# The projections and the scan of a two-layer kernel as one program without a barrier between them

## The chip, the cores and the metric

One Trainium2 chip; the kernel runs on 1 core of it. The metric is the time of one execution on the device in microseconds (us), lower is better. "Engines" are TensorE (PE, its weight loads PEld), VectorE (DVE), ScalarE (ACT), GpSimd (POOL) and SyncE (SP, which here only issues transfers).

## What is computed

Two layers, each a selective state-space mixer (Mamba) and a mixture of experts, both added to the rows `x` (4 x 512 rows of 512). Both mixers read the same context (4 x 512 x 256), so their projections can all be made at the start. For one mixer and batch:

```
x    = in_proj_w @ context                       # 512 channels x 512 positions
u    = silu(conv4(x) + conv_b)                   # 4 taps along the positions
dt, Bm, Cm = split(x_proj_w @ u)                 # 16 + 16 + 16 rows
delta = softplus(dt_proj_w @ dt + dt_proj_b);  A = -exp(A_log)
state = state * exp(delta * A) + (delta * u) * Bm   # 16 states a channel, along the positions
y    = (sum over the states of state * Cm + D * u) * silu(z)
```

z comes from the layer norm of `x`, whose mean and variance are read at the start too. After the first mixer come routing, experts and the second layer.

## The kernel before

`stage_proj` makes the projections: 8 rounds `n` (`ORDER`: layer 1's four batches, then layer 0's), each of 4 channel tiles `j`. For a tile PE multiplies (L267) into banks 0 to 3, ACT copies it with padding (`COPY`, L313) and makes the first tap (L316), DVE the three other taps (L351), ACT the tanh (L305), DVE `u` (L344), and PE adds its share of `x_proj` into `XD` (bank 4, L277). PE runs the products of round n+1 between those of round n. When a round is whole, ACT copies `XD` to `xds` (L301) during the next round, and SP writes its rows to `bc_d`. Behind the last round DVE negates `An` (L361) and makes the layer-norm statistics of the 16 row tiles (`dve_stats`, L633 to L638); POOL makes the reciprocal roots of them (`pool_rstd`, L642 to L649). Then all engines meet: `clear_semaphores` frees the semaphores, with a barrier.

`scan_stage` does 32 groups `g` (mixer, batch, channel tile) of 16 states `i`. For each state ACT makes `dA` (L525), POOL `dBu` (L560), DVE the scan (L607) and then the product with C of the state before (L591), PE sums with an identity matrix (L471) into `YS` (bank 4). POOL and ACT may run a few states ahead of the scan (POOL has two `dBu` buffers). A group's softplus is made during the group before: `dt_proj` on PE (L459), seven activations on ACT (`prep`, steps 0 to 2, L504 to L515) with a table load for `Ln`, `pool_poly` (L536), `dve_pick` (L575), `pool_delta` (L540), `pool_du` (L546). Group 0's has no group before it and stands alone at the start of the stage. SP loads B and C of a batch in four chunks each (L417, L418) out of `bc_d` into `big`, where the context lay. All orders are written out by hand, one program an engine; nothing is reordered. `side` (the class `Beside`) adds the layer-0 experts' work to the scan's steps.

Of the kernel before, what the change touches and what calls it, by code (L numbers as in the profile page):

```python
# [25 lines left out]
ALU = mybir.AluOpType  # L26
ACT = mybir.ActivationFunctionType
# [75 lines left out]
def program(nc, x, ctxT, mix, moe0, moe1, out):  # L103
    ctx = ExitStack()
    with ctx:
# [101 lines left out]
        def stage_proj():  # L207
# [6 lines left out]
            x1_out, bc_out, chain, expa, pad0 = sem("p_x1_out"), sem("p_bc_out"), sem("p_chain"), sem("p_exp_a"), sem("p_pad0")  # L214
            stat_done, mean_done, rstd_done = sem("p_stat"), sem("p_mean"), sem("p_rstd")
            tap_done = sem("p_first_tap_done")
            XP, XD = bank[0:4], bank[4]
            with nc.Block() as block:
                @block.sync
                def _(sp):  # L220
                    def in_proj(k):
                        sp.dma_start(winT[k], mix[k]["in_proj"].rearrange("(c p) e -> p c e", p=P)).then_inc(win_in[k], 16)

                    def ctx(b):
                        sp.dma_start(cx[:, b, :, :], ctxT[b].rearrange("(c p) l -> p c l", p=P)).then_inc(ctx_in[b], 16)

                    def conv(k):
                        sp.dma_start(cw[k][:, :, :], mix[k]["conv_w"].rearrange("(j p) w -> p j w", p=P)).then_inc(par_in[k], 16)
                        sp.dma_start(cbias[k][:, :], mix[k]["conv_b"]).then_inc(par_in[k], 16)
                        sp.dma_start(xprT[k], mix[k]["x_proj"].rearrange("(j p) r -> p j r", p=P)).then_inc(par_in[k], 16)  # L230

                    in_proj(1)
                    ctx(0)
                    conv(1)
                    conv(0)
                    for b in range(1, B):
                        ctx(b)
                    in_proj(0)
                    for k in (0, 1):
                        sp.dma_start(An[k][:, :, :], mix[k]["A_log"].rearrange("(j p) n -> p j n", p=P)).then_inc(late_in[k], 16)  # L240
                        for t_sb, t_d in ((dtb, "dt_b"), (dsk, "D")):
                            sp.dma_start(t_sb[k][:, :], mix[k][t_d]).then_inc(late_in[k], 16)
                    sp.wait_ge(pad0, 4)
                    sp.dma_start(dtwT[0:NR, :], mix[0]["dt_proj"]).then_inc(late_in[0], 16)
                    sp.dma_start(X[:, :, :], x.rearrange("(t p) d -> p t d", p=P)).then_inc(x_in, 16)
                    for n, (k, b) in enumerate(ORDER):
                        if k == 1:
                            sp.wait_ge(u_done, (n + 1) * NJ)
                            sp.dma_start(u1_d[b], Y[:, b * NJ:(b + 1) * NJ, :]).then_inc(u_out[b], 16)
                        sp.wait_ge(xds_done, n + 1)  # L250
                        sp.dma_start(bc_d[b + k * B], xds[NR:NR + 2 * NS, b, :]).then_inc((bc_out, x1_out)[k], 16)
                        if k == 1:
                            sp.dma_start(dt1_d[b], xds[0:NR, b, :]).then_inc(x1_out, 16)
                    sp.wait_ge(bc_out, 16 * B)
                    sp.wait_ge(late_in[0], 64)

                @block.tensor
                def _(pe):
                    def in_proj(n, j):
                        k, b = ORDER[n]  # L260
                        if j == 0 and b == 0:
                            pe.wait_ge(win_in[k], 16)
                        if j == 0 and k == 1:
                            pe.wait_ge(ctx_in[b], 16)
                        at_least(pe, xpad_done, n * NJ + j - 3 if n else 0)
                        for c in range(DC):
                            last = nc.tensor.matmul(XP[j][:, :], winT[k][:, c, j * P:(j + 1) * P], cx[:, b, c, :],  # L267
                                                    start=c == 0, stop=c == DC - 1)
                        last.then_inc(xp_done, 1)

                    def x_proj(n, j):
                        k, b = ORDER[n]
                        if j == 0:
                            at_least(pe, xds_done, n)
                            pe.wait_ge(par_in[k], 48)
                        pe.wait_ge(u_done, n * NJ + j + 1)
                        nc.tensor.matmul(XD[0:48, :], xprT[k][:, j, :], Y[:, b * NJ + j, :], start=j == 0,  # L277
                                         stop=j == NJ - 1).then_inc(xd_done, 1)

                    for j in range(NJ):  # L280
                        in_proj(0, j)
                    for n in range(2 * B):
                        for j in range(NJ):
                            if n < 2 * B - 1:
                                in_proj(n + 1, j)
                            x_proj(n, j)

                @block.gpsimd
                def _(pool):
                    nc.gpsimd.memset(dtwT[:, :], 0.0).then_inc(pad0, 1)  # L290
                    nc.gpsimd.memset(xds[:, :, :], 0.0).then_inc(pad0, 1)
                    pool_rstd(pool, mean_done, rstd_done)

                @block.scalar
                def _(act):
                    def copy_xd(n):
                        k, b = ORDER[n]
                        act.wait_ge(xd_done, (n + 1) * NJ)
                        if n == B:
                            act.wait_ge(x1_out, 32 * B)  # L300
                        nc.scalar.copy(xds[0:48, b, :], XD[0:48, :]).then_inc(xds_done, 1)  # L301

                    def tanh(n, j):
                        act.wait_ge(conv_done, n * NJ + j + 1)
                        nc.scalar.activation(cth[j % 2], cv[j % 2], ACT.Tanh).then_inc(th_done, 1)  # L305

                    act.wait_ge(pad0, 4)
                    act.wait_ge(chain, 4)
                    for n, (k, b) in enumerate(ORDER):
                        for j in range(NJ):  # L310
                            act.wait_ge(xp_done, n * NJ + j + 1)
                            at_least(act, conv_done, n * NJ + j - 1)
                            nc.scalar.copy(xpad[j % 2][:, 3:3 + L], XP[j][:, :]).then_inc(xpad_done, 1)  # L313
                            act.wait_ge(xpad_done, n * NJ + j + 1)
                            at_least(act, u_done, n * NJ + j - 1)
                            nc.scalar.activation(cv[j % 2], xpad[j % 2][:, 0:L], ACT.Identity, bias=cbias[k][:, j:j + 1],  # L316
                                                 scale=cw[k][:, j, 0:1]).then_inc(tap_done, 1)
                            if j:
                                tanh(n, j - 1)
                            if j == 1 and n:  # L320
                                copy_xd(n - 1)
                        tanh(n, NJ - 1)
                        if n == B:
                            for i in range(2):
                                act.wait_ge(late_in[i], (64, 48)[i])
                                nc.scalar.activation(An[i][:, :, :], An[i][:, :, :], ACT.Exp).then_inc(expa, 1)
                    copy_xd(2 * B - 1)

                @block.vector
                def _(dve):  # L330
                    for i in range(2):
                        nc.vector.memset(xpad[i][:, 0:3], 0.0).then_inc(pad0, 1)
                    link = Chain(dve, chain)
                    for k in (1, 0):
                        dve.wait_ge(par_in[k], 48)
                        link(nc.vector.tensor_scalar_mul(cw[k][:, :, :], cw[k][:, :, :], 0.5))
                        link(nc.vector.tensor_scalar_mul(cbias[k][:, :], cbias[k][:, :], 0.5))

                    def u_of(n, j):
                        k, b = ORDER[n]  # L340
                        dve.wait_ge(th_done, n * NJ + j + 1)
                        if k == 0 and j == 0:
                            dve.wait_ge(u_out[b], 16)
                        nc.vector.scalar_tensor_tensor(Y[:, b * NJ + j, :], cth[j % 2], 1.0, cv[j % 2],  # L344
                                                       ALU.add, ALU.mult).then_inc(u_done, 1)
# [1372 lines left out]
```

## Time and profile before

| | before |
|---|---|
| median of 3 runs | 2302.93 us (2299.14 to 2305.75) |
| profiled execution | 2298.09 us, span 2296.4 us |
| PE / DVE / ACT / POOL busy | 1920.6 / 1415.4 / 846.8 / 984.7 us |
| the projections | span's start to 118.5 us |
| statistics, barrier, group 0's softplus | 118.5 to 150.8 us |
| scan | 150.8 us to about 1400 us, experts beside its second half |

The profile is one execution; its spans count from its first instruction. In each 1/40 of the span, DVE is at 0.6 to 0.9 busy or more through the projections and the scan, PE at 0.9 or more in the last third.

### The profile page before, as it was taken

Reading aid. Unit: us, or ns where it says so; the run is one execution under the profiler, and the core shown is the slowest. Engines: PE = TensorE matmul, PEld = TensorE weight load, DVE = VectorE, ACT = ScalarE, POOL = GpSimd, SP = SyncE. Lnnn points to the kernel's source line nnn. Section 1 sums busy time; section 2 is a strip of 40 time slices with the busy share of each in tenths; the row PEclk is TensorE's granted clock in tenths of the full one; section 3 lists DMA queues with packets and bytes.
Section 4 is the critical chain, followed back from the end, with each engine's and each line's share of the span. In section 5 each row is a group of like instructions: output and inputs, shape, how many; then the busy total and the mean of one; then the engine's idle time right before and its main releaser. Section 6 shows DMA issues by size and latency. Waiting matters only on the chain. (4 is left out here: it accounts for less than half of the span.)

```text
span 2296.4 us, 18644 instructions
## 1 busy us (share of the span) xinstructions
PE 1920.6 (84%) x5075; PEld 877.6 (38%) x5075; DVE 1415.4 (62%) x1958; ACT 846.8 (37%) x1372; POOL 984.7 (43%) x873
## 2 busy tenths in 40 slices
PE   8836678789788795489999984999999999999980
PEld 2201133234233341134444433454455555555540
DVE  6869998899898889697888884654111111111114
ACT  5645554545454543655555541110111111111110
POOL 0047866676666665886877762212300000000005
PEclk9958899999899997599999996999999999999995
DMA  5069500302203003568678645113645554455457
GB/s 192 25 233 212 185 13 10 147 14 77 116 13 125 36 10 159 174 210 343 231 253 341 215 166 211 55 38 98 217 157 172 185 176 155 172 184 179 156 194 224
DMA packets 102256, 348.57 MB, mean 152 GB/s; under 512 B 15184, under 2 KB 16208, under 8 KB 84112
## 3 DMA queue, kind: packets, MB, share of 16 engines
q1 hardware_dynamic: 94480, 322.27, 40.9%
q0 software_dynamic: 7680, 25.17, 3.3%
q8 instruction: 41, 0.67, 0.1%
q14 instruction: 55, 0.45, 0.1%
HBM read 284.88 MB, written 62.52 MB: 151 GB/s over the span
## 5 line engine op out<-in xcount | busy, mean ns | idle before, releaser
L560 POOL TENSOR_TENSOR work<-work,big 128x512 f32<-128x512 f32 x512 | 658.1, 1291 | 231.6 <-DVE bank L607 229.9
L471 PE MATMUL bank<-work,ident 128*128 128x512 f32 x928 | 528.5, 683 | 213.2 <-DVE work L591 162.6
L607 DVE TENSOR_TENSOR_SCAN bank<-bank,work 128x512 f32<-128x512 f32 x512 | 625.4, 1221 | 102.3 <-ACT bank L525 54.5
L525 ACT ACTIVATE bank<-work,An 128x512 f32<-128x512 f32 x512 | 346.3, 690 | 305.3 <-DVE work L591 302.3
L471 PEld LDWEIGHTS bank<-work,ident 128*128 128x128 f32 x928 | 173.3, 209 | 512.6 <-DVE work L591 335.1
L591 DVE TENSOR_TENSOR work<-bank,big 128x512 f32<-128x512 f32 x512 | 344.7, 673 | 9.5 <-PE bank L471 9.3
L1636 POOL DMA_INDIRECT W<-ys_d,slot x32 | 32.1, 1002 | 624.7 <-PEq L1623 615.3
L1593 PE MATMUL bank<-Y,big 128*128 128x512 f32 x528 | 258.7, 594 | 0.0
L1183 DVE SCALAR_TENSOR_TENSOR work<-work,bank 128x352 f32<-128x352 f32 (+1 forms) x62 | 35.9, 579 | 300.0 <-ACT work L1173 299.9
L959 PE MATMUL bank<-W,work 128*128 128x512 f32 x384 | 190.8, 600 | 0.0
L1161 ACT COPY work<-bank 128x512 f32<-128x512 f32 x62 | 36.3, 586 | 379.7 <-PE bank L1146 379.7
L1607 PE MATMUL bank<-big,W 128*128 128x512 f32 x352 | 168.3, 592 | 0.0
L1593 PEld LDWEIGHTS bank<-Y,big 128*128 128x128 f32 x528 | 98.6, 191 | 82.7 <-issue 57.5
L1146 PE MATMUL bank<-work 128*128 128x512 f32 (+1 forms) x234 | 114.4, 601 | 4.5 <-DMA work<-down_last 4.5
L1188 DVE SCALAR_TENSOR_TENSOR work<-work,bank 128x352 f32<-128x352 f32 (+1 forms) x62 | 36.0, 580 | 123.3 <-PE bank L1135 123.2
L1135 PE MATMUL bank<-work 128*128 128x352 f32 x312 | 110.7, 460 | 1.5 <-DMA work<-up 1.5
L1544 ACT ACTIVATE work<-bank 128x512 f32<-128x512 f32 x44 | 26.3, 597 | 221.9 <-PE bank L1593 221.9
L1125 PE MATMUL bank<-work 128*128 128x352 f32 x312 | 106.0, 464 | 2.3 <-DMA work<-gate 2.3
L959 PEld LDWEIGHTS bank<-W,work 128*128 128x128 f32 x384 | 72.8, 194 | 84.5 <-issue 84.5
L1498 DVE SCALAR_TENSOR_TENSOR W<-work,bank 128x512 f32<-128x512 f32 x44 | 30.2, 686 | 94.9 <-PE bank L1593 94.7
L1135 PE MATMUL bank<-W,work 128*128 128x512 f32 x184 | 88.2, 618 | 0.5 <-DMA W<-up 0.5
L1607 PEld LDWEIGHTS bank<-big,W 128*128 128x128 f32 x352 | 65.2, 190 | 58.7 <-issue 46.0
(245 smaller groups left out, 2284.5 us busy)
## 6 DMA issues: line engine op xcount, KB each, us to landing
big<-bc_d SPq DMA_DIRECT2D x64, 1024.0 KB, 6.7
work<-gate SPq DMA_DIRECT2D x39, 704.0 KB, 4.1
work<-up SPq DMA_DIRECT2D x39, 704.0 KB, 4.1
W<-gate SPq DMA_DIRECT2D x23, 1024.0 KB, 4.8
W<-up SPq DMA_DIRECT2D x23, 1024.0 KB, 5.4
W<-down SPq DMA_DIRECT2D x23, 1024.0 KB, 5.4
work<-down SPq DMA_DIRECT2D x39, 512.0 KB, 3.7
work<-xs_d SPq DMA_DIRECT2D x62, 256.0 KB, 4.3
```

The lines of the kernel that those rows point to most:

```text
L471: nc.tensor.matmul(YS[:, :], ident[:, :], hC[ring(g * NS + u[0])], start=v == 0, stop=v == len(units[g]) - 1).then_inc(sum_done, 1)
L525: nc.scalar.activation(H[i % 4][:, :], delta[g % 2], ACT.Exp, scale=An[vb // B][:, g % NJ, i:i + 1]).then_inc(dA_done, 1)
L560: nc.gpsimd.tensor_tensor(dBu[i % 2], du[g % 2], Bb[:, i, :], ALU.mult).then_inc(dBu_done, 1)
L591: nc.vector.tensor_tensor(hC[ring(s)], H[i % 4][:, :], Cb[:, i, :], ALU.mult).then_inc(hC_done, 1)
L607: nc.vector.tensor_tensor_scan(H[i % 4][:, :], H[i % 4][:, :], dBu[i % 2], 0.0, ALU.mult, ALU.add).then_inc(scan_done, 1)
L959: ins = nc.tensor.matmul(dst[:, :], at[:, c * P:(c + 1) * P], w[:, c, :], start=c == 0, stop=c == DK - 1)
L1125: ins = nc.tensor.matmul(self.G[:, 0:self.F], self.xT[q][:, c * P:(c + 1) * P], self.wg[:, c, :], start=c == 0, stop=c == DK - 1)
L1135: ins = nc.tensor.matmul(self.U[:, 0:self.F], self.xT[q][:, c * P:(c + 1) * P], self.wu[:, c, :], start=c == 0, stop=c == DK - 1)
L1146: ins = nc.tensor.matmul(self.TB[:, :], self.hT[0:fn, c * P:(c + 1) * P], self.wd[0:fn, c, :], start=c == 0, stop=c == len(self.chunks) - 1)
L1161: nc.scalar.copy(self.yo, self.TB[:, :]).then_inc(S["yo_done"], 1)
L1593: ins = nc.tensor.matmul(dst[:, :], sgu[:, c, u // DK * FS + f * P:u // DK * FS + (f + 1) * P], xTb[b][:, c, :], start=c == 0, stop=c == D ...
L1607: ins = nc.tensor.matmul(down_bank(b, r)[:, :], hT[c][:, r * P:(r + 1) * P], sdw[:, c, :], start=c == 0, stop=c == NF - 1)
```

## The change

The projections are no block of their own any more. `projections()` returns one function for each engine, and the scan's program of that engine calls it first; the block's end, the clearing of semaphores and the barrier go. `XD` moves from bank 4 to bank 5, so that `YS` is free. What orders the two parts now are waits on semaphores of the projections (`free`).

- Group 0's softplus stands inside the projections: `dt_proj(0)` and the three `prep` steps behind round 5 (`mid` on PE and ACT), `pool_poly(0)`, `pool_delta(0)` and `pool_du(0)` right behind POOL's two memsets, `dve_pick(0)` behind round 6.
- The layer-norm statistics stay on DVE between the projections and the scan; `rstds` goes on POOL behind the fourth `dBu` of group 0.
- SP issues the first B and C chunks behind its last `bc_d` write, once every `in_proj` product has read the context; each later batch's chunks wait for that batch's `bc_d` row.

```diff
-            XP, XD = bank[0:4], bank[4]
-            with nc.Block() as block:
+            XP, XD = bank[0:4], bank[5]
...
             def tensor(pe, mid):
                 for n in range(2 * B):
                     for j in range(NJ):
                         if n < 2 * B - 1:
                             in_proj(n + 1, j)
                         x_proj(n, j)
+                    if n == B + 1:
+                        mid(pe)
...
             def gpsimd(pool):
                 nc.gpsimd.memset(xds[:, :, :], 0.0).then_inc(pad0, 1)
-                    pool_rstd(pool, mean_done, rstd_done)
...
             def scalar(act, mid):
                     tanh(n, NJ - 1)
+                    if n == B + 1:
+                        mid(act)
...
             def vector(dve, mid):
                     u_of(n, NJ - 1)
+                    if n == B + 2:
+                        mid(dve)
...
+            def free(eng, name):
+                if name == "sp big":
+                    eng.wait_ge(xp_done, 2 * B * NJ)
+                if name == "sp W":
+                    eng.wait_ge(xd_done, 2 * B * NJ)
+                    eng.wait_ge(u_done, 2 * B * NJ)
...
+                if name == "pe":
+                    eng.wait_ge(xds_done, B + 1)
+                    eng.wait_ge(late_in[0], 64)
+                if name == "act":
+                    eng.wait_ge(chain, 4 + 2 * B * NJ * (NTAP - 2) + 2)
+                if name == "act gates":
+                    eng.wait_ge(rstd_done, 5)
...
             def loads(sp):
+                proj_sp(sp)
+                free(sp, "sp big")
+                sp.wait_ge(bc_out[0], 16)
                 for c in range(4):
                     chunk(0, c)
+                free(sp, "sp W")
                 side.before("sp", sp)
...
             def tensor(pe):
-                dt_proj(0)
+                def first_step(pe):
+                    free(pe, "pe")
+                    dt_proj(0)
+
+                proj_pe(pe, first_step)
...
             def scalar(act):
-                for step in range(3):
-                    prep(0, step)
+                def first_step(act):
+                    for step in range(3):
+                        prep(0, step)
+
+                proj_act(act, first_step)
+                free(act, "act")
...
             def gpsimd(pool):
+                proj_pool(pool)
                 pool_poly(pool, 0)
                 pool_delta(pool, 0)
                 pool_du(pool, 0)
...
                     nc.gpsimd.tensor_tensor(dBu[i % 2], du[g % 2], Bb[:, i, :], ALU.mult).then_inc(dBu_done, 1)
+                    if g == 0 and i == 3:
+                        rstds(pool)
...
             def vector(dve):
-                dve.wait_ge(poly_done, 1)
-                dve_pick(0)
+                def first_step(dve):
+                    dve.wait_ge(poly_done, 1)
+                    dve_pick(0)
+
+                proj_dve(dve, first_step)
+                stats(dve)
...
         stage_setup()
-        stage_proj()
-        clear_semaphores()
         scan_stage(Beside(moe0))
```

ACT where round 5 ends and round 6 begins, in the program before (bank0 and bank1 hold the products of round 6's first tiles, `W` the padded tiles, taps and tanh):

```order
L305 ACTIVATE W<-W 128x512 [waits p_conv_done] x2
L313 COPY W<-bank0 128x512 [waits p_conv_done,p_xp_done]
L316 ACTIVATE W<-W,cbias0,cw0 128x512 [waits p_u_done,p_xpad_done]
L313 COPY W<-bank1 128x512 [waits p_conv_done,p_xp_done]
L316 ACTIVATE W<-W,cbias0,cw0 128x512 [waits p_u_done,p_xpad_done]
L305 ACTIVATE W<-W 128x512 [waits p_conv_done]
```

The same place in the changed program, whose line numbers are 4 lower here (`s_dt_done` is signalled by `dt_proj`, `s_dt_read` by the second activation):

```order
L301 ACTIVATE W<-W 128x512 [waits p_conv_done] x2
L541 ACTIVATE work<-bank4,dtb0 128x512 [waits s_dt_done]
L542 ACTIVATE work<-bank4,dtb0 128x512
L545 ACTIVATE work<-work 128x512 [waits s_dt_read]
L548 ACT_TABLE_LOAD
L548 ACTIVATE work<-work 128x512 [waits s_exp_done]
L549 ACTIVATE work<-work,pbias 128x512
L550 ACTIVATE work<-work,pbias 128x512
L552 ACTIVATE work<-work,pbias 128x512 [waits s_square_done]
L309 COPY W<-bank0 128x512 [waits p_conv_done,p_xp_done]
L312 ACTIVATE W<-W,cbias0,cw0 128x512 [waits p_u_done,p_xpad_done]
```

Seven activations and a table load now stand between the last tanh of round 5 and the first copy of round 6; a second table load follows ahead of round 6's first tanh.

POOL from its memsets to group 0's fifth `dBu`, in the program before (L560 is `dBu`):

```order
L291 MEMSET xds 128x2048
L642 TENSOR_TENSOR rstd<-mv,powers 128x16 [waits p_mean]
L644 TENSOR_TENSOR rstd<-rstd,powers 128x16 [waits p_rstd]
L646 TENSOR_TENSOR rstdx<-rstd,powers 128x16 [waits p_rstd]
L647 TENSOR_TENSOR nbz<-rstd,powers 128x16
L649 TENSOR_TENSOR nbz<-nbz,mv 128x16 [waits p_rstd]
```

and in the changed program (L604 is `dBu`, L579, L583 and L589 are `pool_poly`, `pool_delta` and `pool_du`, L692 to L699 are `pool_rstd`):

```order
L289 MEMSET xds 128x2048
L579 TENSOR_TENSOR work<-work 128x512 [waits s_log_done]
L583 TENSOR_TENSOR work<-work 128x512 [waits s_picked]
L589 TENSOR_TENSOR work<-work,Y 128x512 [waits s_delta_done]
L604 TENSOR_TENSOR work<-work,big 128x512 [waits s_du_done,s_B_in0]
L604 TENSOR_TENSOR work<-work,big 128x512
L604 TENSOR_TENSOR work<-work,big 128x512 [waits s_scan_done] x2
L692 TENSOR_TENSOR rstd<-mv,powers 128x16 [waits p_mean]
```

The five `pool_rstd` instructions moved from ahead of group 0's softplus to behind its fourth `dBu`.

## Rows read from the trace of the kernel before

**Rows 1.** Busy time by stretch: us, then busy (x instructions) of PE, PEld, DVE, ACT, POOL; granted clock, DMA.
```profile
118.50:150.80 32.30, 6.06 (x6) 1.23 (x6) 13.36 (x36) 10.03 (x14) 8.95 (x10) 0.50 0.42 170
...
1400.00:1700.00 300.00, 276.96 (x851) 143.49 (x852) 128.16 (x287) 39.87 (x76) 62.63 (x93) 0.94 0.36 122
1700.00:2296.40 596.40, 535.76 (x1598) 280.51 (x1596) 97.10 (x157) 84.83 (x200) 32.08 (x32) 0.95 0.54 179
```

**Rows 2.** Timeline, last projection to first scan: start us, duration us, instruction, [idle before <-releaser].
```profile
118.82 1.29 DVE L633 BATCH_NORM_STATS2 bst<-X 128x6 f32<-128x512 f32 x2
...
120.48 0.58 ACT L301 COPY xds<-bank 48x512 f32<-48x512 f32 x1 [2.76 <-PE bank L277]
...
131.47 0.18 DVE L638 BATCH_NORM_AGGREGATE mv<-bst 128x2 f32<-128x6 f32 x1
131.73 0.21 POOL L642 TENSOR_TENSOR rstd<-mv,powers 128x16 f32<-128x16 f32 x1 [127.62 <-DVE mv L638]
...
135.51 0.22 POOL L649 TENSOR_TENSOR nbz<-nbz,mv 128x16 f32<-128x16 f32 x1
...
136.69 2.04 PE L459 MATMUL bank<-xds,dtwT 128*128 128x512 f32 x2 [16.24 <-PEq L118]
...
138.77 0.69 ACT L504 ACTIVATE work<-bank,dtb 128x512 f32<-128x512 f32 x1 [17.71 <-PE bank L459]
...
140.71 1.28 ACT L511 ACT_TABLE_LOAD   x1
...
143.77 0.70 ACT L515 ACTIVATE work<-work,pbias 128x512 f32<-128x512 f32 x1
...
145.84 0.73 DVE L575 COPY_PREDICATED work<-work 128x512 f32<-128x512 uint32 x1 [14.20 <-POOL work L536]
...
146.65 1.26 POOL L540 TENSOR_TENSOR work<-work 128x512 f32<-128x512 f32 x1 [0.84 <-DVE work L575]
...
150.77 2.45 DVE L607 TENSOR_TENSOR_SCAN bank<-bank,work 128x512 f32<-128x512 f32 x2 [4.20 <-POOL work L560]
```

**Rows 3.** Timeline where round 5 of the projections ends and round 6 begins.
```profile
91.47 0.57 ACT L313 COPY W<-bank 128x512 f32<-128x512 f32 x1
...
92.45 1.06 PE L277 MATMUL bank<-Y,W 128*48 128x512 f32 x2
...
92.92 2.99 DVE L351 SCALAR_TENSOR_TENSOR W<-W,cw 128x512 f32<-128x512 f32 x4 [0.63 <-ACT W L316]
93.39 0.81 ACT L316 ACTIVATE W<-W,cbias,cw 128x512 f32<-128x512 f32 x1
...
93.44 1.98 PE L267 MATMUL bank<-big,W 128*128 128x512 f32 x4
...
95.28 0.63 ACT L305 ACTIVATE W<-W 128x512 f32<-128x512 f32 x1 [1.08 <-DVE W L351]
```

**Rows 4.** Timeline of PE in the last round of the projections.
```profile
112.75 1.94 PE L277 MATMUL bank<-Y,W 128*48 128x512 f32 x2 [1.79 <-DVE Y L344]
```

**Rows 5.** Timeline of POOL and DVE in the scan, operands of both in SBUF.
```profile
198.08 1.27 POOL L536 TENSOR_TENSOR work<-work 128x512 f32<-128x512 f32 x1
...
198.99 0.91 DVE L880 SCALAR_TENSOR_TENSOR work<-work 128x512 f32<-128x512 f32 x1
...
199.30 3.07 POOL L560 TENSOR_TENSOR work<-work,big 128x512 f32<-128x512 f32 x2
```

**Rows 6.** Timeline of group 0 of the scan.
```profile
152.08 2.48 POOL L560 TENSOR_TENSOR work<-work,big 128x512 f32<-128x512 f32 x2 [0.20 <-DVE bank L607]
...
157.15 1.22 DVE L607 TENSOR_TENSOR_SCAN bank<-bank,work 128x512 f32<-128x512 f32 x1
...
163.78 1.23 DVE L607 TENSOR_TENSOR_SCAN bank<-bank,work 128x512 f32<-128x512 f32 x1 [1.39 <-ACT bank L525]
```

**Rows 7.** DMA issues of the first B chunk and the last C chunk: KB each, us to landing.
```profile
big<-bc_d SPq DMA_DIRECT2D x1, 1024.0 KB, 4.6
...
big<-bc_d SPq DMA_DIRECT2D x1, 1024.0 KB, 18.9
```

More of the change, by code:

```diff
@@ L213, in stage_proj @@
             th_done, u_done, xd_done, xds_done = sem("p_th_done"), sem("p_u_done"), sem("p_xd_done"), sem("p_xds_done")
[L214 removed]
+            x1_out, chain, expa, pad0 = sem("p_x1_out"), sem("p_chain"), sem("p_exp_a"), sem("p_pad0")
+            bc_out = [sem(f"p_bc_out{b}") for b in range(B)]
             stat_done, mean_done, rstd_done = sem("p_stat"), sem("p_mean"), sem("p_rstd")
@@ L216, in stage_proj @@
             tap_done = sem("p_first_tap_done")
-            XP, XD = bank[0:4], bank[4]
-            with nc.Block() as block:
[L219 to L278, printed above, removed]
-                    for j in range(NJ):
[L281 to L291, printed above, removed]
-                    pool_rstd(pool, mean_done, rstd_done)
[L294 to L345, printed above, removed]
-                    for n, (k, b) in enumerate(ORDER):
-                        for j in range(NJ):
-                            dve.wait_ge(tap_done, n * NJ + j + 1)
-                            for w in range(1, NTAP):
-                                ins = nc.vector.scalar_tensor_tensor(cv[j % 2], xpad[j % 2][:, w:w + L], cw[k][:, j, w:w + 1],
-                                                                     cv[j % 2], ALU.mult, ALU.add)
-                                if w < NTAP - 1:
-                                    link(ins)
-                                if w == 1 and j:
-                                    u_of(n, j - 1)
-                            ins.then_inc(conv_done, 1)
-                        u_of(n, NJ - 1)
-                    dve.wait_ge(expa, 2)
-                    for k in range(2):
-                        link(nc.vector.tensor_scalar_mul(An[k][:, :, :], An[k][:, :, :], -1.0))
-                    dve.wait_ge(x_in, 16)
-                    dve_stats(dve, stat_done, mean_done)
@@ new lines, in tensor, with in_proj, x_proj @@
+            def tensor(pe, mid):
+                def in_proj(n, j):
+                    k, b = ORDER[n]
+                    if j == 0 and b == 0:
+                        pe.wait_ge(win_in[k], 16)
+                    if j == 0 and k == 1:
+                        pe.wait_ge(ctx_in[b], 16)
+                    at_least(pe, xpad_done, n * NJ + j - 3 if n else 0)
+                    for c in range(DC):
+                        last = nc.tensor.matmul(XP[j][:, :], winT[k][:, c, j * P:(j + 1) * P], cx[:, b, c, :],
+                                                start=c == 0, stop=c == DC - 1)
+                    last.then_inc(xp_done, 1)
+                def x_proj(n, j):
+                    k, b = ORDER[n]
+                    if j == 0:
+                        at_least(pe, xds_done, n)
+                        pe.wait_ge(par_in[k], 48)
+                    pe.wait_ge(u_done, n * NJ + j + 1)
+                    nc.tensor.matmul(XD[0:48, :], xprT[k][:, j, :], Y[:, b * NJ + j, :], start=j == 0,
+                                     stop=j == NJ - 1).then_inc(xd_done, 1)
+                for j in range(NJ):
+                    in_proj(0, j)
+                for n in range(2 * B):
+                    for j in range(NJ):
+                        if n < 2 * B - 1:
+                            in_proj(n + 1, j)
+                        x_proj(n, j)
+                    if n == B + 1:
+                        mid(pe)
@@ L366, in scan_stage @@
+            return sync, tensor, scalar, gpsimd, vector, stats, rstds, free, bc_out
         def scan_stage(side):
+            proj_sp, proj_pe, proj_act, proj_pool, proj_dve, stats, rstds, free, bc_out = projections()
             GROUPS = 2 * B * NJ
@@ L437, in loads @@
                         zeros(i)
+                    if g == 0 and i == 2:
+                        free(sp, "sp rows of layer 1")
                     if g == 13 and i == 0:
@@ L528, in scalar @@
                         prep(g + 1, i - y_at[g] - 3)
+                    if g == 1 and i == 0:
+                        free(act, "act gates")
                     if vb <= B:
```

108 lines of the change are left out of this document (107 added, 1 removed).

## The prediction

> **What bounds the kernel now.** I read the busy time by stretch first. The change touches only the first 180 us or so. The stretch between the projections and the scan is 32.3 us long, and no engine is busy in more than 13.4 us of it [rows 1]: there a chain runs from engine to engine, and any of its links that moves under other work is a gain. The timeline shows the links [rows 2]. DVE goes from the last projection straight into the statistics (118.82) and ends them at 131.65 (131.47 + 0.18). POOL makes the roots (131.73 to 135.73), the engines meet, PE multiplies `dt_proj` at 136.69, ACT makes the softplus from 138.77 to 144.47, then `pool_poly`, `dve_pick`, `pool_delta`, `pool_du` and the first `dBu` follow one another, and the first scan starts at 150.77. From the end of the statistics to the first scan DVE does one 0.73 us instruction in 19.1 us.
>
> In the projections the bound is the DVE-ACT pair: four taps of DVE take 2.99 us back to back, and at a round's end DVE waits only 0.63 us for ACT's next tap [rows 3]. So what I put on ACT or DVE there costs nearly its whole length. In the scan DVE sets the pace too, about 1.75 us a state: from state 4 at 157.15 to state 7 at 163.78 without its 1.39 us wait is 5.24 us for three [rows 6].
>
> **What goes.** Everything between the end of the statistics and the first scan: 150.77 - 131.65 = **19.1 us**, if by the statistics' new end dA and dBu of state 0 are there. Barrier and freeing of semaphores lie in it. The check: the first B chunk is issued behind ACT's last copy of `xds` (ends 121.06 before [rows 2]), say 0.5 us later, and lands 4.6 us after its issue [rows 7]; `dBu` takes 1.27. That is 127.5 in the old clock, where the statistics end at 131.65, and both move together: 4 us to spare. ACT negates nothing, it waits for DVE's `An` (before the statistics) and has its first dA ready even sooner. The last C chunk lands 18.9 us after its issue, and state 12 comes 21 us into the scan; it is issued some 7 us ahead of the scan, so no chunk is late. Behind the chunks SP's queue goes on (shared weights, zero rows) as before, somewhat earlier; nobody waits for those in the first groups.
>
> **What the softplus costs inside the projections.** ACT's order is fixed: behind the tanh of round 5's last tile it now waits for `dt_proj(0)`, and round 6's first copy and tap stand behind seven activations. PE does `x_proj` of that tile at 92.45 as before, and where the next product started, at 93.44 [rows 3], it starts `dt_proj`. Two passes of 128 x 512 took 1.06 us with PE at its full pace (2.04 at half clock [rows 2], not the case here, PE has been at 4 passes in 1.98). So ACT begins at 94.54. Its block is 5.70 us long (138.77 to 144.47, with the table load of 1.28). The copy comes at 94.54 + 5.70 - 0.10 (such instructions overlap by that much) = 100.14 instead of 91.47: **+8.7 us**, and DVE's first tap moves by as much, since it waits for ACT.
>
> Then the table load back for the tanh. ACT's second tap ended at 94.20 and the tanh started at 95.28, idle 1.08 [rows 3]; the load of 1.28 fills that gap and ends 0.2 later: **+0.2 us**. Ahead of the scan no load is left, but that one was hidden.
>
> `dve_pick` is 0.73 us in a 0.63 us wait behind round 6: **+0.1 us**.
>
> `pool_poly` runs from 100.3 to 101.6, while DVE waits. But `pool_delta` and `pool_du` start when `dve_pick` ends, just as DVE goes through the taps of round 7, whose two tensor inputs lie in SBUF. In the scan such a pair shows what happens [rows 5]: DVE's L880 starts at 198.99 while POOL works until 199.35, and takes 0.91 us; the next two of POOL, started at 199.30, take 3.07 where two took 2.48 [rows 6]. So one stands while the other works. Least is no cost at all (POOL starved, which can wait); most is twice a POOL instruction, 2.5 us. DVE's taps come back to back and each waits for a signal, so POOL gets its turn twice; I take **+2.4 us**. The nearest DVE row would give about 0.2 each, because it met only the end of a POOL instruction.
>
> The Trainium skill speaks against the change here: "SBUF — State Buffer", section "Who interferes with whom", has an exclusive lock between a VectorE instruction with two SBUF inputs and a GpSimd instruction that reads SBUF, and whoever is second blocks fully. The trace agrees as far as it goes. By that rule the cost is two whole POOL instructions, by the DVE row alone 0.4 us; the sum would be 2 us lower by the latter.
>
> **What the roots cost inside the scan.** `pool_rstd` keeps POOL for 4.0 us (131.73 to 135.73 [rows 2]) behind the fourth `dBu`, and `dBu` of state 4 queues behind it. Count from the first scan (150.77 before): POOL ends its fourth `dBu` at 154.56, +3.8 [rows 6], is free at +7.8, and `dBu` 4 is there at +9.1; the scan of state 4 ran at +6.4 and now runs at +9.2. State 7 then comes 5.2 later, at +14.4. Before it came at +13.0, after a wait of 1.39 us for ACT, which was busy with group 1's softplus. ACT's work up to dA 7 hangs on products of states before 4 only, so it goes on while DVE waits for POOL, and the two waits lie over each other: 14.4 - 13.0 = **+1.4 us**. Bounds: 0 if POOL gets ahead, 2.8 if ACT is held too.
>
> **Sum.** -19.1 + 8.7 + 0.2 + 0.1 + 2.4 + 1.4 = **-6.3 us**. Everything behind hangs on the first scan in the same order, so I carry it whole to the end. Against the profiled execution, 2298.09, that is 2291.8. The median of the runs lies 4.8 us higher (2302.93), so the time to expect is 2302.93 - 6.3 = **2296.6 us**. 0.3% of the time, what a measurement tells from no change, is 6.9 us: the forecast sits just inside of it.
>
> **Rivals.**
>
> A. *Both hidden costs are nil.* POOL's two instructions find gaps, and the roots disappear in POOL's slack. For it: POOL has some idle time at each state. Against: the rows of the lock, and 4.0 us is far more than the slack of a state. It gives -19.1 + 9.0 = -10.1, 2292.8.
>
> B. *TensorE falls to half clock in the stall.* PE has nothing to do from 94.5 until round 6's first copy is through, about 6 us. In round 7, where it had little to do, two passes took 1.94 instead of 1.06 [rows 4, 3], as at the granted clock of 0.50 (1.2 GHz instead of 2.4) of the stretch behind it [rows 1]. If it stayed there through round 6, a tile would need 2 x (1.98 + 0.9..1.06), some 5.8 us, four of them 23.3 against 13.1 of DVE's round; PE would be about 10 us late at the end, and ACT's copy of `xds` for round 6, behind the second tap pair of round 7, has about 4 us of room: +6, 2302.6. Against: PE has dense work there, and only rounds without it show 1.94. A short dip at the round's start costs nothing, since its products are needed a round later.
>
> C. *Slower: the clock of the last third.* From 1400 us on PE is busy 812.7 us and sets the end, at a granted clock of 0.94 to 0.95 [rows 1]. Its dips depend on where idle and busy stretches fall, and all of it moves by 6 us. One hundredth of clock there is 812.7 / 95 = 8.6 us. The gain is gone at 0.7 hundredths less; slower by 0.3% needs 13.2 us, 1.5 hundredths. For it: the three runs of before already differ by 6.6 us. Against: the stage starts at its own barrier with the same program.
>
> D. *The change doesn't bring the loads forward.* The title says B and C load when the context has been read. In SP's program they stand behind the last `bc_d` write, so they start with the end of the projections. It changes nothing in the sum, which doesn't need them sooner; only if the chunk were 4 us later would it be the next thing late.
>
> **How the numbers follow.** Forecast 0.50 (2294 to 2299), A 0.22, B 0.13, C 0.08, the rest 0.07 spread. The bounds of the two uncertain terms give -10.1 (2292.8) to -4.8 (2298.1); the median moves by a microsecond or two by itself, and the top takes in B: **2291.5 to 2302.5**. Faster by over 0.3% means under 2296.0: A, two fifths of the forecast's own chance and a little of the rest, 0.44. Within: 0.48. Slower: C, 0.08.
>
> **What the new profile would show.** A gap in DVE of about 9.3 us (8.7 + 0.6) behind round 5 with ACT's softplus in it, starting some 3 us after the last tanh; taps of over 1 us in round 7 beside POOL's L583 and L589; no gap of DVE between the statistics and the first scan, which starts near 143.1 us; a 2.8 us wait of the scan of state 4 for POOL, and none for ACT at state 7. If the gap behind round 5 were much longer or the first scan waited for a chunk, the prediction would be wrong in its main term; if the first scan starts at 143 and the end isn't 6 us earlier, it would be wrong in carrying it whole.

## The result, and the profile after

| | before | changed |
|---|---|---|
| median | 2303.66 us (20 runs, 2293.69 to 2311.81) | 2295.89 us (20 runs, 2290.88 to 2303.29) |
| profiled execution's span | 2296.4 us | 2290.6 us |
| PE / DVE / ACT / POOL busy | 1920.6 / 1415.4 / 846.8 / 984.7 us | 1921.8 / 1416.1 / 847.0 / 985.8 us |

The ratio is 0.997, 95% interval 0.9958 to 0.9982: shorter by 0.3%, about 7 us, and the interval leaves out 1. The busy times are the same to within 1.2 us, so what changed is waiting.

DVE in the changed kernel from the end of round 5 to the scan's eighth state (timeline: start us, duration us, instruction, [idle before <-releaser]):

```profile
101.69 2.99 DVE L348 SCALAR_TENSOR_TENSOR W<-W,cw 128x512 f32<-128x512 f32 x4 [9.37 <-ACT W L312]
...
114.29 0.74 DVE L621 COPY_PREDICATED work<-work 128x512 f32<-128x512 uint32 x1
115.01 4.75 DVE L348 SCALAR_TENSOR_TENSOR W<-W,cw 128x512 f32<-128x512 f32 x4
...
142.23 0.18 DVE L688 BATCH_NORM_AGGREGATE mv<-bst 128x2 f32<-128x6 f32 x1
143.18 2.35 DVE L657 TENSOR_TENSOR_SCAN bank<-bank,work 128x512 f32<-128x512 f32 x2 [0.76 <-issue]
...
152.25 1.23 DVE L657 TENSOR_TENSOR_SCAN bank<-bank,work 128x512 f32<-128x512 f32 x1 [2.72 <-POOL work L604]
...
157.42 1.22 DVE L657 TENSOR_TENSOR_SCAN bank<-bank,work 128x512 f32<-128x512 f32 x1
```

These answer to [rows 2, 3, 6]. Between the statistics' end and the first scan there were 19.1 us, now there are 0.77. In their place stands a gap of 9.37 us behind round 5, where 0.63 us stood. The four taps at round 7's start take 4.75 us instead of 2.99. The first scan starts 7.59 us earlier than before (143.18 against 150.77), and of this 1.23 us is given back by state 7: it runs 14.24 us behind the first, before 13.01.

ACT and PE in the gap (timeline):

```profile
94.64 0.69 ACT L541 ACTIVATE work<-bank,dtb 128x512 f32<-128x512 f32 x1 [3.04 <-PE bank L492]
...
96.58 1.28 ACT L548 ACT_TABLE_LOAD   x1
...
100.25 0.56 ACT L309 COPY W<-bank 128x512 f32<-128x512 f32 x1
...
100.86 3.78 PE L264 MATMUL bank<-big,W 128*128 128x512 f32 x4 [6.26 <-ACT W L309]
...
102.99 1.28 ACT L301 ACT_TABLE_LOAD   x1
104.29 0.63 ACT L301 ACTIVATE W<-W 128x512 f32<-128x512 f32 x1
```

DVE's gap is ACT's softplus and the `dt_proj` ahead of it: the copy that stood at 91.47 [rows 3] stands at 100.25. PE idles for 6.26 us, and its next four passes take 3.78 us where four took 1.98 [rows 3]. The granted clock by stretch (us, busy (x) of PE, PEld, DVE, ACT, POOL; clock, DMA share, GB/s) shows that this is short:

```profile
100.90:104.70 3.80, 3.74 (x4) 1.13 (x4) 2.92 (x4) 3.74 (x5) 0.79 (x1) 0.50 0.00 0
104.70:115.00 10.30, 9.15 (x20) 2.69 (x20) 8.96 (x13) 6.47 (x12) 0.00 (x0) 1.00 0.03 6
...
119.00:131.00 12.00, 7.52 (x8) 0.94 (x8) 10.78 (x20) 5.57 (x9) 0.00 (x0) 0.50 0.02 5
```

It is at 0.50 (1.2 GHz) for those passes and back at 1.00 (2.4 GHz) behind them; no instruction of DVE waits longer for it. In the last round, where PE has two passes at a time, it is at 0.50 again (third line).

### The profile page after: what moved, and what is told of

Read it like the earlier page. It is cut to its first block and busy times, and to the rows that moved or that the text cites. A ratio compares the mean times of both kernels' runs of the same rounds, so it can differ in the third digit from the quotient of the medians.

```text
span 2290.6 us, 18624 instructions
## 1 busy us (share of the span) xinstructions
PE 1921.8 (84%) x5075; PEld 876.0 (38%) x5075; DVE 1416.1 (62%) x1958; ACT 847.0 (37%) x1372; POOL 985.8 (43%) x873
## 5 line engine op out<-in xcount | busy, mean ns | idle before, releaser
L604 POOL TENSOR_TENSOR work<-work,big 128x512 f32<-128x512 f32 x512 | 657.6, 1290 | 253.9 <-DVE bank L657 233.9
```

The source lines that it names most:

```text
L604: nc.gpsimd.tensor_tensor(dBu[i % 2], du[g % 2], Bb[:, i, :], ALU.mult).then_inc(dBu_done, 1)
```

## The experiments

All runs are read at two places, because a single execution's span says little here (see the table behind them): where the first scan starts, and where DVE makes group 1's pick, in state 11 of group 0, when the start's waits are over. That pick stands at 172.38 us before and at 166.00 in the changed kernel. Before an edit acts, executions already differ by up to half a microsecond: DVE's first tap of round 6, ahead of everything that pool_later, roots_split and early_chunks edit, comes at 101.69 us in the changed kernel and at 101.46, 101.65 and 101.24 in these three.

**softplus_back** puts group 0's softplus behind the projections again, and keeps the rest.

```diff
-                    if n == B + 1:
-                        mid(act)
...
                 copy_xd(2 * B - 1)
+                mid(act)
...
-                    if n == B + 2:
-                        mid(dve)
...
                 stats(dve)
+                first_step(dve)
```

> The changed kernel, but ACT's three softplus steps of group 0 behind its last copy of xds and the pick on DVE behind the statistics; one program without a barrier, roots in the scan, bank 5 as they are. My theory (the softplus costs ACT and DVE about 10.8 us inside the projections, 8.8 stall, 0.2 table load, 1.8 lock): the last u comes 10.8 us earlier, the statistics end at 131.6, behind them pick 0.7, delta, du and dBu 3 x 1.3, so the first scan starts at about 136.5 instead of 143.2 and the kernel takes 6 to 7 us less than the changed one, about 2289. Rival (the place of the softplus makes no difference, because the chain behind the statistics grows by what the rounds lose): within 1 us of the changed kernel.

```profile
120.96 0.68 ACT L538 ACTIVATE work<-bank,dtb 128x512 f32<-128x512 f32 x1
...
125.94 0.70 ACT L549 ACTIVATE work<-work,pbias 128x512 f32<-128x512 f32 x1
...
131.56 0.69 DVE L618 COPY_PREDICATED work<-work 128x512 f32<-128x512 uint32 x1
132.33 1.26 POOL L580 TENSOR_TENSOR work<-work 128x512 f32<-128x512 f32 x1 [4.33 <-DVE work L618]
...
136.45 2.45 DVE L655 TENSOR_TENSOR_SCAN bank<-bank,work 128x512 f32<-128x512 f32 x2 [4.20 <-POOL work L601]
```

It took 2291.48 us at the median (6 runs), ratio to before 0.9948 (0.9935 to 0.9962). ACT makes the softplus under DVE's statistics (timeline above). The first scan waits 4.20 us for POOL and still starts 6.73 us earlier than in the changed kernel: the statistics end 10.8 us earlier (131.64 against 142.41), and 4.0 us of that go to the chain that is back. So moving the softplus into the rounds cost more than the chain that it took from the scan's start. The time gained on the changed kernel is 5.1 us by the ratios, against 6 to 7 expected; the two intervals overlap (table below), so this rests on the position in the trace.

Against the kernel before, this variant starts its first scan 14.3 us earlier, with the same rounds. No run parts the barrier from what stood with it in the chain. The rows of before add up to the amount, which is an estimate: from the statistics' end to the end of the roots 4.08 us, from there to `dt_proj` behind the barrier 0.96, from `dt_proj` to the pick 9.15 [rows 2], together 14.2. Without the barrier ACT makes the softplus beside the statistics.

**pool_later** makes POOL wait for the last `u` before its `pool_delta`.

```diff
+                if name == "pool":
+                    eng.wait_ge(u_done, 2 * B * NJ)
...
                 pool_poly(pool, 0)
+                free(pool, "pool")
                 pool_delta(pool, 0)
```

> The changed kernel, but POOL waits with delta and du of group 0 until DVE has made the last u. My theory (DVE and POOL block each other where both read two operands from SBUF): the four taps of round 7 take 2.99 us again instead of 4.75, delta and du take 1.26 each instead of 1.76 and 1.59, they cost nothing beside the statistics, and the first scan starts at about 141.4 instead of 143.2. Rival (something else slows round 7, for example PE at the lower clock): taps still 4.75.

```profile
114.77 2.99 DVE L348 SCALAR_TENSOR_TENSOR W<-W,cw 128x512 f32<-128x512 f32 x4
...
127.13 1.48 DVE L360 TENSOR_SCALAR An<-An 128x64 f32<-128x64 f32 x2
...
127.29 1.26 POOL L585 TENSOR_TENSOR work<-work 128x512 f32<-128x512 f32 x1 [25.83 <-DVE Y L341]
...
128.64 1.27 POOL L591 TENSOR_TENSOR work<-work,Y 128x512 f32<-128x512 f32 x1
128.64 1.29 DVE L686 BATCH_NORM_STATS2 bst<-X 128x6 f32<-128x512 f32 x2
```

The taps are back at 2.99 us, so the 1.76 us were POOL's doing. But the two `An` instructions behind the last `u`, 0.42 us otherwise, now meet `pool_delta` (L585) and take 1.48 us. The first scan starts at 142.24, 0.94 us earlier and not 1.8; 0.23 of that was there before round 6, and the rest is 1.76 less 1.06: part of the cost moved with the POOL instruction. `pool_du` (L591) lies beside the statistics and costs nothing: two of them take 1.29 us, as they do alone [rows 2].

**roots_split** spreads `pool_rstd` over three places of group 0 (behind `dBu` 3, 8 and 11).

```diff
-                    if g == 0 and i == 3:
-                        rstds(pool)
+                    if g == 0 and i in (3, 8, 11):
+                        rstds(pool, (3, 8, 11).index(i))
```

> The changed kernel, but pool_rstd in three parts: the addition behind the dBu of state 3, the power behind that of state 8, the other three behind that of state 11. My theory (two waits of DVE lay over each other in group 0): the 2.7 us wait of state 4 for POOL goes, the 1.4 us wait of state 7 for ACT comes back, and state 7 starts 13.0 us behind state 0 instead of 14.2; the power costs about 0.2 at state 9. In all 1.0 to 1.2 us less. Rival (ACT is also held by POOL): 2.7 us less, no wait at state 7.

```profile
156.03 1.23 DVE L657 TENSOR_TENSOR_SCAN bank<-bank,work 128x512 f32<-128x512 f32 x1 [1.39 <-ACT bank L566]
...
159.71 1.23 DVE L657 TENSOR_TENSOR_SCAN bank<-bank,work 128x512 f32<-128x512 f32 x1 [0.15 <-POOL work L604]
...
162.16 1.23 DVE L657 TENSOR_TENSOR_SCAN bank<-bank,work 128x512 f32<-128x512 f32 x1 [0.64 <-POOL work L604]
```

State 4's wait is gone and state 7's 1.39 us for ACT is back, as the theory of two waits lying over each other says: state 7 is 12.90 us behind the first scan. The power alone (2.94 us) then makes states 9 and 10 wait, and at the pick only 0.39 us are left of the gain, where 1.0 to 1.2 were expected.

**early_chunks** issues the first four chunks of B and C behind round 5.

```diff
                 for n in range(2 * B):
...
+                    if n == B + 1:
+                        early(sp)
```

> The changed kernel, but SP issues B and C of batch 0 behind the bc_d write of round 5, as soon as the last in_proj product has read the context (about 114.6 us), ahead of the writes of rounds 6 and 7. The plain view is that earlier loads can only help: no change, or a gain if the first scan waited for them. My theory: the first scan waits for the statistics only, so nothing is gained, and the two dBu that POOL may make ahead now come at 119 to 122 us, in the middle of DVE's taps, where they block each other as delta and du did: the last u comes 1.5 to 2.5 us later and the first scan starts at 144.7 to 145.7 instead of 143.2.

```profile
120.01 4.09 DVE L350 SCALAR_TENSOR_TENSOR W<-W,cw 128x512 f32<-128x512 f32 x3
...
120.33 3.23 POOL L608 TENSOR_TENSOR work<-work,big 128x512 f32<-128x512 f32 x2 [2.23 <-DMA big<-bc_d]
```

POOL now gets its B in round 7 and makes two `dBu` against DVE's taps: three of these take 4.09 us where three took 2.20, and the two products 3.23 instead of 2.48. The first scan starts at 144.53 us, 1.35 later, from a round 6 that began 0.45 earlier: the same operands earlier cost 1.8 us, inside the 1.5 to 2.5 expected; the start itself lies just under the 144.7 to 145.7 expected.

**marks_first** tests the 0.76 us that the trace calls issue ahead of the first scan.

```diff
+                side.before("dve", dve)
                 proj_dve(dve, first_step)
                 stats(dve)
-                side.before("dve", dve)
```

> The changed kernel with one edit: the ten semaphore increments that VectorE issues between the statistics and the first scan are issued at its start instead, where it waits for its first data. Nothing is left out. My theory puts the 0.76 us that the trace shows there as issue down to them: the first scan should begin 0.1 to 0.2 us behind the last statistic's end, so that the first scan and state 7 come 0.7 to 0.8 us earlier (142.4 and 156.7 us), and the first memsets at the start come 0.8 us later, without effect. The rival says that the 0.76 us is what a scan costs when it follows statistics (its two first operands' releases, or fetching of the scan's code): then it stays, and the first scan begins at 143.2 us.

```profile
142.13 0.18 DVE L688 BATCH_NORM_AGGREGATE mv<-bst 128x2 f32<-128x6 f32 x1
142.22 2.32 DVE L657 TENSOR_TENSOR_SCAN bank<-bank,work 128x512 f32<-128x512 f32 x2
```

The gap is gone, state 7 runs at 156.45 and the pick at 165.03, 0.97 us earlier (0.10 of that was there before round 6). DVE's first instruction comes at 2.75 us instead of 1.91, with nobody waiting. The expectation miscounts: `Beside` has DVE mark nine semaphores, not ten. They take about 0.8 us of DVE's program in either place.

**under_stats, stats_in_gap and all_hidden** put work where the trace of the changed kernel shows waits. The first has ACT's part where softplus_back has it, and the pick between two statistics:

```diff
-                stats(dve)
+                stats(dve, at=13, hook=first_step)
```

> The first group's softplus stays in the same program, but ScalarE runs it behind its last copy of xds instead of behind round 5's tanh, and VectorE does the pick between two of its statistics, ahead of tile 13's. Nothing is left out. My theory says that the changed kernel paid for the place of the softplus (in the one stretch where VectorE waits for ScalarE) and that the same work under the statistics, where VectorE has its own work and ScalarE none, costs almost nothing. Then the rounds run as in the kernel before: last u near 117.8 us, softplus on ScalarE from about 121 to 127, pick on VectorE near 129, and the first scan near 133.2 us, 10 us earlier than the changed kernel's 143.18 (9.1 for the stall that is gone, 1.8 for taps that no longer meet GpSimd, less 0.8 for the pick), while GpSimd's delta, du and first product lie beside the statistics. Carried to the end: 8 to 10 us less than the changed kernel, about 2287 us against 2296. The rival says that the statistics lengthen beside GpSimd's delta and du as the taps did, or that ScalarE is not free there: then the first scan comes 1 to 5 us later than that.

The second keeps the softplus where the change put it, and fills DVE's gap with 11 of the 16 statistics (with pool_later's wait and the early chunks):

```diff
+                    if n == B + 1:
+                        gap(dve)
...
-                proj_dve(dve, first_step)
-                stats(dve)
+                proj_dve(dve, first_step, lambda dve: stats(dve, 0, 11))
+                stats(dve, 11)
```

> The changed kernel with the order of its softplus kept, but VectorE does 11 of the 16 tiles' statistics in the gap behind round 5, the first four chunks of B and C load behind round 5 too, and GpSimd waits for the last u before it begins delta. Nothing is left out. My theory says that the 9.37 us gap of VectorE is a real hole in the path to the first scan, so work of the same path put into it shortens the path by its whole length: last u near 126.8 us, the five statistics left, and the first scan near 132.5 us, about 10 us earlier than the changed kernel's 143.18; time about 2286 us. The rival is that something else (GpSimd's delta, du and product, which now lie behind the last u: about 5.3 us plus the lock on VectorE's statistics) becomes what the first scan waits for: then it begins at 133.5 to 135 us and the time is 2287 to 2289 us.

The third:

```diff
+                    if n == 2 * B - 1:
+                        mid(act, (0, 1))
                     tanh(n, NJ - 1)
+                    if n == 2 * B - 1:
+                        mid(act, (2,))
...
-                proj_dve(dve, first_step)
-                stats(dve)
                 side.before("dve", dve)
+                proj_dve(dve, lambda dve, t: stats(dve, t, t + 1))
+                stats(dve, 7, at=11, hook=first_step)
```

> Every piece put where its engine waits by the trace of the changed kernel. ScalarE does the two steps of the softplus that need no other table in its wait of the last round, and the third with its table load behind the last tanh; VectorE does seven of the statistics one per round, in the 0.7 us by which it waits in each, and the pick ahead of tile 11's; the chunks load behind round 5; the root of the variances is split between three products of GpSimd. Nothing is left out. My theory, by which each engine's idle time on the path to the first scan is what can be won and nothing else is, expects: rounds hardly longer than in the kernel before (last u near 118.5 us), the first scan near 129 us, 14 us earlier than the changed kernel's 143.18, and 15 us less at the end, about 2281 us. The rival says that the rounds' waits are not free (a statistic of 1.2 us in a wait of 0.7 us lengthens the round by 0.5 us, and TensorE's clock falls with its longer waits): then last u comes 3 to 5 us later and the gain on the changed kernel is 10 to 12 us.

DVE in under_stats, behind the pick:

```profile
128.92 0.70 DVE L619 COPY_PREDICATED work<-work 128x512 f32<-128x512 uint32 x1
...
131.84 0.18 DVE L689 BATCH_NORM_AGGREGATE mv<-bst 128x2 f32<-128x6 f32 x1
133.82 2.45 DVE L655 TENSOR_TENSOR_SCAN bank<-bank,work 128x512 f32<-128x512 f32 x2 [1.80 <-POOL work L602]
```

From the pick's start to the first scan are 4.9 us (delta, du, `dBu` on POOL one behind another), and the statistics behind it cover only 3.1: the pick stood a tile or two too late. The 0.6 us by which it missed 133.2 lie there. The rival's stretched statistics did not come: the two that meet `pool_delta` (129.69 to 130.95) take 0.68 and 0.69 us, as elsewhere. The median is 2288.47 us, for 2287 expected.

DVE in stats_in_gap, from the gap to the first scan:

```profile
100.00 0.69 DVE L695 BATCH_NORM_STATS2 bst<-X 128x6 f32<-128x512 f32 x1
100.61 0.16 DVE L698 BATCH_NORM_AGGREGATE mv<-bst 128x2 f32<-128x6 f32 x1
101.58 2.99 DVE L350 SCALAR_TENSOR_TENSOR W<-W,cw 128x512 f32<-128x512 f32 x4 [0.80 <-ACT W L314]
...
127.25 1.48 DVE L364 TENSOR_SCALAR An<-An 128x64 f32<-128x64 f32 x2
...
133.67 2.35 DVE L667 TENSOR_TENSOR_SCAN bank<-bank,work 128x512 f32<-128x512 f32 x2 [0.76 <-issue]
```

Of the hole 0.80 us is left, so the statistics fill 8.6 of it. The first scan starts 9.5 us earlier than in the changed kernel; of the rest 0.7 is pool_later's gain, which this run has too, and 0.1 was there before round 6. The 1.2 us missing to 132.5 are mostly the `An` instructions beside POOL, 1.06 us, as in pool_later. The numbers (133.67, and a median of 2287.90 us) lie in the rival's ranges, but its wait isn't there: POOL ends the first `dBu` near 131.4, and the 0.76 us ahead of the scan are the semaphore increments.

DVE in all_hidden, a statistic in round 7's wait, and the start of the scan:

```profile
116.69 0.69 DVE L692 BATCH_NORM_STATS2 bst<-X 128x6 f32<-128x512 f32 x1
117.30 0.17 DVE L695 BATCH_NORM_AGGREGATE mv<-bst 128x2 f32<-128x6 f32 x1
117.47 0.69 DVE L345 SCALAR_TENSOR_TENSOR Y<-W 128x512 f32<-128x512 f32 x1
...
122.60 0.73 DVE L628 COPY_PREDICATED work<-work 128x512 f32<-128x512 uint32 x1 [0.86 <-POOL work L586]
...
127.53 2.45 DVE L664 TENSOR_TENSOR_SCAN bank<-bank,work 128x512 f32<-128x512 f32 x2 [0.18 <-POOL work L611]
```

The rival fell: a statistic and its aggregate take 0.78 us here, not the 1.2 that it assumed, and fit a wait of 0.7. The last `u` comes at 117.47, against 117.76 in the kernel before, and both are 24.8 us behind round 6's first tap. ACT's first two steps fit its wait of the last round, and the first scan starts at 127.53 us, where 129 was expected. This run changes several things at once; it shows their sum, not the share of each.

All kernels, in us; the first three columns and "rest" are of the profiled execution, the time is the median; "rest" is the span less the start of the last scan's row in DVE's timeline, "gain" is 1 less the ratio, times 2303.66, each ratio is to the runs of before that belong to it:

| kernel | first scan | pick in group 0 | last scan | rest | time (runs) | gain by the ratio (interval) |
|---|---|---|---|---|---|---|
| before | 150.77 | 172.38 | 1376.80 | 919.6 | 2303.66 (20) | |
| changed | 143.18 | 166.00 | 1368.42 | 922.2 | 2295.89 (20) | 6.9 (4.1 to 9.7) |
| softplus_back | 136.45 | 159.28 | 1364.32 | 919.3 | 2291.48 (6) | 12.0 (8.8 to 15.0) |
| pool_later | 142.24 | 165.06 | 1372.28 | 921.8 | 2295.78 (1) | |
| roots_split | 143.13 | 165.61 | 1376.78 | 920.9 | 2299.44 (1) | |
| early_chunks | 144.53 | 167.36 | 1376.40 | 922.1 | 2300.23 (1) | |
| marks_first | 142.22 | 165.03 | 1375.99 | 922.3 | 2300.01 (1) | |
| under_stats | 133.82 | 156.67 | 1366.59 | 923.0 | 2288.47 (5) | 16.4 (12.9 to 19.8) |
| stats_in_gap | 133.67 | 156.51 | 1357.80 | 922.8 | 2287.90 (4) | 15.0 (10.6 to 19.4) |
| all_hidden | 127.53 | 150.13 | 1351.70 | 923.5 | 2276.89 (5) | 24.4 (20.3 to 28.8) |

The pick is 6.4, 13.1, 15.7, 15.9 and 22.3 us earlier than before in the five timed kernels, and their times are shorter by 6.9, 12.0, 16.4, 15.0 and 24.4: each within its interval. What is won at the start is whole at the end. all_hidden (ratio 0.9894, expected 2281 us) beats both kernels.

The same table shows what one execution can't tell. From the pick to the last scan are 1201.3 (stats_in_gap) to 1211.2 us (roots_split) in the changed kernel and its eight variants, whose programs are the same behind that pick. Against the changed kernel, marks_first is 0.97 us ahead at that pick and 6.2 us behind from 770 to 1340 us, 7.6 at the last scan, and most of this comes in jumps of 1 to 2 us. The jump of 2 us to 6.2 lies in one group, between 724 and 764 us of the changed kernel, 728 and 770 of marks_first. Ten microseconds of the same work there, in the changed kernel (same columns as above):

```profile
734.00:744.00 10.00, 6.25 (x13) 1.90 (x11) 6.39 (x8) 2.13 (x4) 2.92 (x4) 0.95 0.29 121
```

and in marks_first:

```profile
738.00:748.00 10.00, 6.65 (x12) 2.33 (x11) 5.81 (x7) 2.21 (x4) 2.67 (x3) 0.79 0.33 116
```

The granted clock is 0.95 in the one and 0.79 in the other, and in that group marks_first's DVE waits 0.45, 1.11 and 0.93 us for PE's banks where the other waits once, 0.61 us (a wait of 4.3 us stands in both). This holds for this one jump: that the others, and the spread of the other variants, come from the clock too isn't shown. Why the clock falls in one run and not in the next wasn't tested.

## Why the prediction was right

It gave 2296.6 us (2291.5 to 2302.5), and 2295.89 was measured. That the two times lie 0.7 us apart is in part luck: the forecast was a gain of 6.3 us, the medians differ by 7.8 and the ratio gives 6.9 (4.1 to 9.7). What bears out the working are its terms.

| term | forecast | measured | by |
|---|---|---|---|
| statistics to first scan | -19.1 | -18.4 | 0.77 us left; marks_first |
| softplus in ACT's order | +8.7 | +8.8 | copy 91.47, now 100.25 |
| table load back | +0.2 | +0.2 | tanh 104.29 |
| `dve_pick` | +0.1 | below 0.1 | round 6's last `u` 9.00 later, round 7's first tap 9.01 |
| POOL beside the taps | +2.4 | +1.8 | taps 4.75 against 2.99; pool_later |
| roots in group 0 | +1.4 | +1.2 | 14.24 against 13.01; roots_split |
| sum | -6.3 | -6.4 | state 7 at 157.42, before 163.78 |

**Two misses cancel.** I took the whole stretch as removed and did not look at what else DVE issues there: nine semaphore increments, which before lay behind the pick, under DVE's wait for POOL, now stand bare (0.76 us). Against that the lock of POOL on the taps was mis-sized by 0.6 us. I took it as nearly two whole POOL instructions (2.4 of 2.5 us); it measured 1.8. By the Trainium skill, "SBUF — State Buffer", section "Who interferes with whom", the second of such a pair waits for the first. The trace agrees with the waiting. POOL's two (115.11 to 116.87 and 116.96 to 118.55 us) take 1.76 and 1.59 us instead of 1.26, and of DVE's four taps the two in the middle take 0.89 longer each than the 0.75 of the others:

```profile
115.79 1.64 DVE L348 SCALAR_TENSOR_TENSOR W<-W,cw 128x512 f32<-128x512 f32 x1
...
117.47 1.63 DVE L348 SCALAR_TENSOR_TENSOR W<-W,cw 128x512 f32<-128x512 f32 x1
```

Each of them ends 0.55 or 0.56 us behind the end of the POOL instruction that it met. What the forecast left out is that the pairs overlap at their edges: POOL's first had waited while the first tap ran, and the second of a pair is done 0.55 us behind the first, not its own 0.75. The row that it read, L880 [rows 5], shows the same distance: it ends at 199.90, POOL's at 199.35.

**"Two waits lie over each other"** held at state 7, and roots_split shows both halves of it. But the 1.4 us were not there to be won: with the roots spread out, POOL is late at states 9 and 10.

**Carried whole to the end.** The profiled span is 5.8 us shorter, the ratio says 6.9, and the five timed kernels bear it out. Inside the one profiled pair it can't be followed: the lead in the scan wanders between 3.3 and 8.4 us.

**Rivals.** A (hidden costs nil) is refuted by the stretched taps and the 2.72 us wait. B: the fall of PE's clock came, but ended with the fourth pass, as its "against" said. C: the rest behind the scan is 2.6 us longer than before in the profiled pair, which eats part of the 8.4 us by which the scan ends earlier; but such a spread is seen between all the runs (919.3 to 923.5), so nothing of it is put down to the change. The clock of the last third, on which C rested, is the same in the pair: 0.94 and 0.95 before [rows 1], and 0.94 (1391.6 to 1691.6 us) and 0.95 (from there to the end) in the changed kernel. D: the loads did not come with the reading of the context but with the end of the projections, as it said (first issue at 132.27; before, behind the barrier, at 136.65). POOL's first `dBu` ran at 137.04 to 138.3, 4 us ahead of the statistics' end, the spare time that the forecast had worked out. early_chunks shows that loading earlier by itself does harm here.

## What to carry to other kernels

A barrier costs what it keeps from starting: itself it took about 1 us here, but the chain behind it could not lie beside the statistics. Where the chain goes instead decides how much is kept. Move work to where its engine waits and the engine that sets the pace does not wait for it: the softplus in ACT's place between two rounds cost 8.8 us, and under DVE's statistics the same instructions held up nobody. When one engine must wait, give it work of the same path (the statistics filled 8.6 us of the 9.4 us hole), and for each operation that is made free earlier, ask what it will run beside: here each GpSimd instruction cost DVE 0.9 to 1.1 us beside the taps and beside `An`, and nothing beside the statistics.

## What the runs showed of the hardware that was not expected

- Nine semaphore increments on DVE take 0.76 to 0.84 us, 0.09 each, and the timeline shows them only as idle time named issue.
- The contention of POOL and DVE is not for three-operand taps alone: two TENSOR_SCALAR of 128x64, 0.42 us together, took 1.48 us beside `pool_delta` (pool_later, stats_in_gap). BATCH_NORM_STATS2 took its 0.69 us beside the same instructions (pool_later, under_stats).
- After 6.26 us without work PE ran four passes at 0.50 and was at 1.00 directly behind them, whereas in the last round, where it had two passes at a time, both ran at half pace (1.94 us for two [rows 4]; 0.50 from 119 to 131 us in the changed kernel).
- Between executions of nearly the same program the scan stage varies by some 10 us; in the one jump of 2 us shown above, TensorE's granted clock was 0.79 in one run and 0.95 in the other.
